# First projections as a pipeline with doubled buffers, norms on ScalarE, q's split on GpSimd, parts of q and k written to DRAM once

## The reference

```python
q = split_heads(x @ Wq + bq)             # 16 heads of width 8
k = split_heads(x @ Wk + bk)
v = split_heads(x @ Wv + bv)
scores = einsum('bhid,bhjd->bhij', q, k)
rel = einsum('bhid,pd->bhip', q, rel_key)      # 256 relative places
logits = where(causal, (scores + bias from rel) * scale, -inf)
out = einsum('bhij,bhjd->bhid', softmax(logits), v)
```

## Time and profile before

| | |
|---|---|
| median of three runs | 4478.52 us |
| the profiled execution | 4480.28 us |
| its span | 4478.4 us |
| PE busy, share of the span | 4185.3 us, 93% |
| DVE busy | 3697.2 us, 83% |
| ACT busy | 3591.3 us, 80% |
| POOL busy | 2342.0 us, 52% |
| mean granted TensorE clock | 0.968 |

### The profile page before, as it was taken

How to read it: one execution, slowest core, us unless ns; L and a number is a source line. 1 busy time by engine, 2 the same in 40 slices (tenths; PEclk the granted TensorE clock), 3 DMA queues, 4 the chain that set the end, 5 groups by cost and what they waited for, 6 DMA issues and landing times. The chain is left out here.

```text
span 4478.4 us, 137304 instructions
## 1 busy us (share of the span) xinstructions
PE 4185.3 (93%) x44000; PEld 2964.7 (66%) x44000; DVE 3697.2 (83%) x8420; ACT 3591.3 (80%) x6842; POOL 2342.0 (52%) x2840
## 2 busy tenths in 40 slices
PE   4899999966999999999999999999999999999994
PEld 2466666643777777777777777777777777777773
DVE  6688888876888888888888888888888888888884
ACT  1799998944888888888888888888888888888882
POOL 1000000016766666666766666666666666666661
PEclk7899999977999999999999999999999999999996
DMA  6777777722111111111111111111111111111111
GB/s 224 219 234 230 228 226 229 234 77 70 37 45 41 44 37 38 45 41 45 35 40 44 41 45 35 43 41 41 45 35 43 40 41 45 36 42 40 45 40 49
DMA packets 258776, 359.63 MB, mean 80 GB/s; under 512 B 44404, under 2 KB 216156, under 8 KB 257884
## 3 DMA queue, kind: packets, MB, share of 16 engines
q1 hardware_dynamic: 258140, 351.55, 26.0%
HBM read 151.19 MB, written 93.34 MB: 55 GB/s over the span
## 5 line engine op out<-in xcount | busy, mean ns | idle before, releaser
L1369 PE MATMUL la_ps<-la_Wqkv,la_xsT 128*128 (+1 forms) x2304 | 1195.1, 614 | 6.4 <-DVE la_rsk L1083 3.5
L1026 POOL TENSOR_TENSOR la_rt<-la_rt,la_rn 128x1024 f32<-128x1024 f32 x384 | 722.9, 1904 | 27.5
L1083 DVE TENSOR_TENSOR la_rsq<-la_ps,la_tab 128x1024 f32<-128x1024 f32 x384 | 469.3, 1222 | 104.5 <-ACT la_sq L1227 101.4
L1227 ACT ACTIVATE la_sq<-la_ps 128x512 f32<-128x512 f32 x768 | 454.5, 596 | 90.1 <-PE la_ps L1369 28.2
L1090 DVE TENSOR_REDUCE la_ssum<-la_sq 128x8 f32<-128x512 f32 x768 | 502.3, 673 | 24.0 <-issue 24.0
L1404 PEld LDWEIGHTS la_ps<-la_kT,la_qB 128*64 128x64 f32 x12288 | 391.3, 138 | 146.1 <-issue 145.8
L1369 PEld LDWEIGHTS la_ps<-la_Wqkv,la_xsT 128*128 128x128 f32 x2304 | 378.1, 191 | 150.4 <-issue 109.7
L1083 DVE TENSOR_TENSOR la_rsk<-la_ps,la_tab 128x1024 f32<-128x1024 f32 x384 | 465.1, 1211 | 4.7 <-ACT la_sq L1227 4.4
L1435 PEld LDWEIGHTS la_ps<-la_Wo,la_oT 128*128 128x128 f32 x3072 | 366.7, 192 | 131.1 <-issue 130.3
L1404 PE MATMUL la_ps<-la_kT,la_qB 128*64 128x64 f32 x12288 | 434.1, 224 | 0.0
L475 POOL COPY at_vh<-V 128x64 f32 (+1 forms) x64 | 15.2, 238 | 785.6 <-PE at_ps L674 784.8
(11 more groups left out here) (168 smaller groups left out, 10272.7 us busy)
## 6 DMA issues: line engine op xcount, KB each, us to landing
at_band<-skew_scratch SPq DMA_DIRECT2D x64, 1536.0 KB, 7.3
la_vs<-la_v SPq DMA_DIRECT2D x192, 384.0 KB, 3.5
skew_scratch<-at_R SPq DMA_DIRECT2D x64, 1024.0 KB, 6.7
la_vs<-la_v SPq DMA_DIRECT2D x192, 128.0 KB, 3.4
la_Wqkv<-in_wqkv SPq DMA_DIRECT2D x28, 384.0 KB, 3.3
kt_scratch<-pr_k SPq DMA_DIRECT2D x24, 384.0 KB, 3.2
qt_scratch<-pr_q SPq DMA_DIRECT2D x24, 384.0 KB, 4.1
at_qh<-qt_scratch SPq DMA_DIRECT2D x64, 144.0 KB
```

The source lines that it names most:

```text
L1026: e.tensor_tensor(heads(rt, w), heads(rt, w), wide(rn[:, w * H:(w + 1) * H], D), ALU.mult)\
L1083: e.tensor_tensor(dst.rearrange("p f (h d) -> p f h d", d=D), ps[:, c % 2, :].rearrange("p (h d) -> p h d", d=D).unsqueeze(1).to_broadcast ...
L1227: e.activation(sq[:, c % 2, :], ps[:, c % 2, :], ACT.Square).then_inc(sq_ev.sem, 1)
L1369: e.matmul(ps[:, c % 2, :], xsT[:, m * P:(m + 1) * P], Wqkv[:, ds(layer(n) % 2, 1), c * 512:(c + 1) * 512], start=True, stop=True)\
```

## The change

The DRAM scratches hold each part once (k: three; q: five, the first two again behind the third, so that any three in a row are a rotation). A step writes them with 3 + 5 DMAs of 128 KB. The 72-row tiles are built at the read: the source of `qh` is three overlapping blocks of 24 rows at a step of one part, the source of `kh` the same block of 24 rows three times (step 0). Size and destination of the loads stay.

The projections lose the rounds; all 8 steps are written out with lags 0 to 3, every buffer, PSUM bank and norm has two copies, and waits look two steps back. ScalarE normalises (scale and bias from the statistics; `mr`, minus mean by root, is one new small VectorE instruction) and copies q and k out twice each, as f32 and as the first bf16 part. GpSimd does the rest of q's split, VectorE the rest of k's. Each sequence of x has a semaphore of its own, and the weights another.

```diff
-    qt_d = nc.dram_tensor("qt_scratch", [PARTS, PARTS, P, B * S], BF16).ap()
-    kt_d = nc.dram_tensor("kt_scratch", [PARTS, PARTS, P, B * S], BF16).ap()
+    qt_d = nc.dram_tensor("qt_scratch", [H_A, 2 * PARTS - 1, D_A, B * S], BF16).ap()
+    kt_d = nc.dram_tensor("kt_scratch", [H_A, PARTS, D_A, B * S], BF16).ap()
...
         @block.sync
         def _(e):
...
+            for n in range(STEPS):
+                u, to = n % 2, ds(n * G * P, G * P)
+                e.wait_ge(k3_ev.sem, k3_ev.v(n))
+                for p in range(PARTS):
+                    e.dma_start(kt_d[:, p, :, to], k3[:, u, p, :]).then_inc(k_out[u].sem, 16)
+                e.wait_ge(q3_ev.sem, q3_ev.v(n))
+                for p in range(2 * PARTS - 1):
+                    e.dma_start(qt_d[:, p, :, to], q3[:, u, p % PARTS, :]).then_inc(q_out[u].sem, 16)
...
         @block.gpsimd
         def _(e):
...
+            for i in range(STEPS + 3):
+                for n, u in steps(i, 3):
+                    e.wait_ge(q_ev.sem, q_ev.v(n))
+                    e.tensor_tensor(qf[:, u, :], qf[:, u, :], q3[:, u, 0, :], ALU.subtract).then_inc(c_q.sem, 1)
+                    e.wait_ge(c_q.sem, c_q.v(n, 1))
+                    e.tensor_tensor(q3[:, u, 1, :], qf[:, u, :], unit[:].to_broadcast([P, G * P]), ALU.mult)\
+                        .then_inc(c_q.sem, 1)
+                for n, u in steps(i, 0):
+                    ln[u].root(e, n // 2)
+                for n, u in steps(i, 3):
+                    e.wait_ge(c_q.sem, c_q.v(n, 2))
+                    e.tensor_tensor(q3[:, u, 2, :], qf[:, u, :], q3[:, u, 1, :], ALU.subtract).then_inc(q3_ev.sem, 1)
...
         @block.scalar
         def _(e):
...
+            for i in range(STEPS + 2):
+                for n, u in steps(i, 1):
+                    e.wait_ge(mr_ev.sem, mr_ev.v(n))
...
+                        act = e.activation(xh[:, u, g, :], tile(n, g), ACT.Identity, bias=mr[:, u, g, :],
+                                           scale=ln[u].st[:, g, 8:9])
+                for n, u in steps(i, 2):
+                    e.wait_ge(q_mm.sem, q_mm.v(n))
...
+                    if n >= 2:
+                        e.wait_ge(q3_ev.sem, q3_ev.v(n - 2))
+                        e.wait_ge(q_out[u].sem, q_out[u].v(n // 2 - 1))
+                    e.activation(qf[:, u, :], ps[:, BANK_Q + u, :], ACT.Identity, bias=bqs[:, 0:1], scale=-SC_A)
+                    e.activation(q3[:, u, 0, :], ps[:, BANK_Q + u, :], ACT.Identity, bias=bqs[:, 0:1], scale=-SC_A)\
+                        .then_inc(q_ev.sem, 1)
...
             def heads_in(n, m):
                 e.wait_ge(s_mm.sem, s_mm.v(n - RING_A))
                 hd = n % HEADS_A
-                row, col = ds(hd % H_A * D_A, D_A), ds(hd // H_A * S, S)
-                for dst, src in ((qh, qt_d), (kh, kt_d)):
-                    e.dma_start(dst[:, m, :], src.rearrange("a b p c -> (a b) p c")[:, row, col])\
+                col = hd // H_A * S
+                for dst, src, step in ((qh, qt_d, D_A * B * S), (kh, kt_d, 0)):
+                    head = src[ds(hd % H_A, 1), 0:PARTS, :, ds(col, S)].rearrange("h a d c -> (h a d) c")
+                    e.dma_start(dst[:, m, :], bass.AP(head.tensor, head.offset, [[step, PARTS]] + list(head.ap)))\
                         .then_inc(qk_in[m % 2].sem, 16)
```

More of the change, by code:

```diff
@@ L203, in first_projections @@
[L203 to L207, removed]
-        block = t.block()
[L209 to L218, removed]
@@ L220, in tiles_of @@
-        def tiles_of(i):
-            first = i * G + i // (TB // G) + 1
-            return [X[:, ds(first + g, 1), :] for g in range(G)]
+        x_in, w_in, s_in = [t.sem(f"x{b}") for b in range(B)], t.sem("win"), t.sem("in")
+        s_z, s_f, s_sk, s_bk = (t.sem(n) for n in ("z", "f", "sk", "bk"))
+        ln = [Norm(t, f"ln{u}", G) for u in range(2)]
+        mr_ev, xh_ev, t_mm, xhT_ev = t.mark("mr"), t.mark("xh"), t.mark("t"), t.mark("xhT")
+        q_mm, k_mm, v_mm = t.mark("qm"), t.mark("km"), t.mark("vm")
@@ new lines, in first_projections, with steps @@
+        q_ev, k_ev, v_ev = t.mark("qe"), t.mark("ke"), t.mark("ve")
+        q3_ev, k3_ev, rel3_ev = t.mark("q3"), t.mark("k3"), t.mark("r3")
+        q_out, k_out = [t.mark(f"qo{u}", 80) for u in range(2)], [t.mark(f"ko{u}", 48) for u in range(2)]
+        rel_out = t.mark("ro", 16)
+        c_q, c_k, c_rel = t.mark("cq", 2), t.mark("ck", 2), t.mark("cr", 2 * PARTS - 2)
+        block = t.block()
+        BANK_T, BANK_Q, BANK_K, BANK_V = 0, 2, 4, 6
+        def steps(i, lag):
+            if 0 <= i - lag < STEPS:
+                yield i - lag, (i - lag) % 2
@@ L234, in _ @@
             e.dma_start(relT[:], a["relT"]).then_inc(s_in, 16)
-            e.wait_ge(rel3_ev.sem, rel3_ev.v(0))
-            e.dma_start(rel_d.rearrange("a p c -> p a c"), rel3[:]).then_inc(rel_out.sem, 16)
+            for b in range(1, B):
+                x_loaded(b)
             e.wait_ge(s_f, 2)
@@ L264, in _ @@
                             pattern=[[-1, BAND]], channel_multiplier=1).then_inc(s_f, 1)
[L265 to L270, removed]
+            e.memset(unit[:], 1.0).then_inc(s_f, 1)
+            for b in range(B):
+                e.memset(X[:, b * ZERO_SLOT, :], 0.0).then_inc(s_z, 1)
+            e.wait_ge(s_f, 3)
+            for i in range(STEPS + 3):
[10 more added lines that the diff above has]
+                    e.tensor_tensor(q3[:, u, 2, :], qf[:, u, :], q3[:, u, 1, :], ALU.subtract).then_inc(q3_ev.sem, 1)
@@ L272, in _ @@
+            e.wait_ge(s_z, B)
         @block.vector
         def _(e):
[L274 to L281, removed]
@@ L342, in body @@
[L342 to L343 removed]
+                for n, u in steps(i, 2):
+                    if n >= 2:
+                        e.wait_ge(v_ev.sem, v_ev.v(n - 2))
                     for g in range(G):
[L345 to L346 removed]
+                        mm = e.matmul(ps[:, BANK_V + u, cols(g)], xhT[:, u, cols(g)], Wv[:], start=True, stop=True)
```

167 lines of the change are left out of this document (88 added, 79 removed).

## The result

The changed kernel takes 4639.7 us (median of 4 runs, 4625.6 to 4649.5), the kernel before 4478.2 beside it: ratio 1.0358 (95% interval 1.0326 to 1.0390), slower by 3.6%. Forecast were 4672 us, with a range of 4530 to 4755. The profiled execution has a span of 4630.7 us, 152.3 more than before.

A forecast was written before the change was run, and what follows sets the result against it. Each head's turn was taken as bound by a wait for loads landing behind the 1.5 MB band, 12.65 us. 4480.3 - 31 (projections) + 1.4 (first pair) + 192 (landing) + 31 (clock) = 4673.7, less 1.8: 4672 us, range 4530 to 4755.

The forecast's parts named there:

- The ring: Steady attention, per head: band issue, 8.46 us to the loads' landing, 4.19 us to the next band issue, 12.65 in all.
- the three engines: Loads of q and k: with 3 source blocks, three DMA engines carry what nine did, 96 KB each a head, not 32.
- Projections: Start of the kernel: the new order ends at 73.2 us in place of 104.3, a gain of 31 us (bounds 38 and 21).
- the two-buffer loop: Projections: copy, GpSimd's split, five issues and landing take 11.4 to 12.1 us every two steps, 5.7 to 6.1 a step.
- The shared port: Projections: VectorE and GpSimd share a port, so their work stands in a row, 5.3 to 6.0 us a step.
- First pair: Attention's start: the first pair of loads lands 1.4 us later, 3.8 us for 96 KB where SyncE's issues paced 2.4.
- Later landing: Steady attention: 64 KB more per engine delay each head from the third on by 3.1 us, 192 us over 62 heads.
- the prediction's own sign: Test in the steady attention: wrong in size if the loads' landing moves by other than 2.5 to 3.7 us.
- Clock: TensorE in the attention: idle lowers its clock in about one head in five, 0.5 us a head, 31 us in all.
- The rival with a fall in every head: TensorE's clock falls in every attention head, 62 x 2.4 in place of 62 x 0.5: 4790 us; chance 0.07.
- the loads stay spread: Rival on the attention's loads: the turn stays at 12.65 us and only the projections count, 4448 us; chance 0.12.
- different threes: Rival: the two loads fall on different engines, 48 KB on each, 0.6 to 0.9 us a head, 4498 us; chance 0.07.

The follow-up runs named there:

- e8: The kernel of e1 with one row of padding behind each block of 8 rows of the DRAM scratch; 4634.2 us, ratio 1.0349 to the kernel before.
- e11: The kernel of e1 with three buffers in place of two for the projections' split parts q3 and k3; 4448.7 us, ratio 0.9923 to the kernel before.
- e6: The kernel of e1 with q's split in the projections moved from GpSimd to VectorE; 4481.0 us, ratio 0.9996 to the kernel before.
- e4: The changed kernel with 12 useless transposes on TensorE ahead of each head's wait for the loads; 4582.6 us, ratio 1.0225 to the kernel before.
- e9: The changed kernel with each head's loads put ahead of the band in SyncE's queue, three-block loads kept; 4444.9 us, ratio 0.9916 to the kernel before.
- e1: The changed kernel with each head's q and k read by three DMAs of 24 rows in place of one; 4457.0 us, ratio 0.9938 to the kernel before.
- e14: The kernel of e1 with 24 useless one-column VectorE instructions at the head of the program; 4484.3 us, ratio 1.0007 to the kernel before.
- e15: The kernel of e6 with 24 useless one-column VectorE instructions at the head of the program; 4451.4 us, ratio 0.9935 to the kernel before.
- e3: The changed kernel with q's load left at three blocks and k's read by three DMAs of 24 rows; 4501.9 us, ratio 1.0043 to the kernel before.

## Why the prediction was right, and where its sizes were off

The mechanism held. The ring, the three engines and the sign come out as written, and e8 shows the cause by one row of padding. Of the change itself 193 us were forecast (4672 less 4478.5). The terms, against the measured 160 us (ratios) or 152 us (spans):

- **Projections, -31.** Measured -28.9. The first q copy came at 14.24 us in place of 15.9, the last at 62.09, where 15.9 + 7 x 6.6 gives 62.1, so the steps took 6.8 us. The tail was taken as 11.1 us and was 13.4: q's parts were ready at 67.4, but SyncE's queue issues k's three writes first, at 68.00, so that q's five start at 69.88, and they took 3.2 us in place of 2.5 (rows above). Of the reasons for a step the two-buffer loop is the one that a run shows (e11). The shared port slowed VectorE (e6), but its part in the step isn't separated.
- **First pair, +1.4.** Measured +3.2: from `at_relD` to the first product 6.6 us before (110.93) and 9.8 after (85.28). I paced the old pair by SyncE and the new one by one load; both loads of the pair share the three engines.
- **Later landing, 3.1 us a head, 192 in all.** Measured 1.84 to 1.99 us a head (10.40 and 10.55 less 8.56), 62 x 1.9 = 118. This is the step that failed in size: I multiplied the 64 extra KB by a rate, and left the old 32 KB at their crowded price. The right sum takes each case whole: 96 KB at a third of 74 GB/s are 3.9 us, 32 KB at 17.4 KB/us are 1.8 us, so 2.1 us. The trace's records of single DMA packets bear it out: the loads' 144 packets of 2 KB run from 5.7 to 7.7 us behind the band's issue before and from 5.8 to 9.9 in the changed kernel (medians of 50 turns), 4.1 us in place of 2.0. By the prediction's own sign, a landing that moves by other than 2.5 to 3.7 us, it was wrong in size here.
- **Clock, 0.5 us a head, 31 in all.** Measured by e4 1.04 a head, about 65. What failed is how often the clock falls: I took one fall in five heads at 2.4 us each, and there are 34 in 63 turns, at some 1.9 us each (65 / 34). The low level outlasts the work that I counted, as the 10.2 us at 0.50 show, and a fall costs less than I counted, it seems because TensorE then waits less for the loads. It falls so often although TensorE stands still for only 72 of 720 us, 1.6 us a turn and at most 2.5 at a time, where I had about 3. The rival with a fall in every head was nearer in how often than its 0.07 says, though its 2.4 us a head were too much.

The two errors were of opposite sign: 3.6 us a head forecast, 2.9 measured. That 4672 lies within 0.7% of the result is partly luck: the landing was 74 us too high and the clock 34 too low, and together the 62 heads came out 45 us above what 2.87 us a turn give. The prediction's own bounds don't give the range that it states for its side either: 2.3 to 4.2 us a head with the bounds of the projections make about 4585 to 4720, not 4600 to 4745. The result lies in both.

The rivals: that the loads stay spread is excluded by 74 GB/s and e8, different threes by the size of the delay (48 KB on an engine, 24 packets in place of 16, would have cost 0.5 us). What the prediction did not see is the cheap way out, the order of the queue: it took the loads' place behind the band as given, and e9 shows that the three engines ahead of the band are nearly harmless.

## What to carry to other kernels

Count the engines of every DMA on a ring, and count them from the slowest dimension of the source too: a scratch that is written once and read back as three copies may save writes and lose engines. Then look at what stands ahead of it in its queue; a small load that something waits for goes ahead of a large one that nothing waits for yet. And when a late transfer idles TensorE in each turn, price the clock over the stretch behind the stall, not only over the work that the stall delays.

## What the runs showed of the hardware that was not expected

- Ten waits of VectorE in a late loop took 2.4 or 4.7 us each, depending on 24 instructions at the head of its code (e1, e6, e14, e15): 27 to 31 us, as much as the new projections gain. A comparison of two kernels can be off by so much through this alone. The Trainium skill (Runtime: NRT & Kernel Launch, Instruction fetch mechanics) has instructions streamed in blocks, and a taken branch to a block not at hand waits for its fetch. That fits ten returns of a loop; no run here shows the fetch itself, nor why 24 instructions decide.
- GpSimd and VectorE in order of time in the changed kernel:

```profile
47.67 1.15 POOL L281 TENSOR_TENSOR pr_q<-pr_qf,pr_q 128x512 bf16<-128x512 f32 x1
```
```profile
47.74 1.11 DVE L319 SCALAR_TENSOR_TENSOR pr_mr<-pr_ln_stats 128x4 f32<-128x4 f32 x1 [0.90 <-POOL pr_ln_stats L124]
48.77 0.68 DVE L325 TENSOR_TENSOR pr_k<-pr_kf,pr_k 128x512 bf16<-128x512 f32 x1
```

  Four columns took 1.11 us on VectorE, which ended with the GpSimd instruction that had begun 0.07 us earlier. Over 20 to 75 us such instructions take 1.04 us in the mean in e1 and 0.16 in e6, where GpSimd has no split. The cast, with one input, was slower beside GpSimd too (0.59 in place of 0.42 us mean), which the prediction had counted in, at its undisturbed 0.43 us.
- The landing of loads behind a 1.5 MB band grew by 0.054 to 0.062 us for each 2 KB packet on the fullest engine above 16 (e3, e4), and ahead of the band 96 KB an engine cost almost nothing (e9).
- SyncE took 0.89 us to issue a load of 24 rows whose source is 3 padded blocks of 8, and 0.46 where the same rows touch (2.68 and 1.39 us for three, e8 and e1).
